# The bucket one-hots of the block building, made by GpSimd in place of VectorE

## The reference

```python
def _hypergraph_conv(x, node_idx, edge_idx, D_inv, B_inv, W, b):
    xt = x @ W
    e = B_inv[:, None] * segment_sum(xt[node_idx], edge_idx, NUM_HYPEREDGES)
    out = D_inv[:, None] * segment_sum(e[edge_idx], node_idx, NUM_NODES)
    return out + b
h = relu(_layernorm(x));  x = x + conv(relu(conv(h, W1, b1)), W2, b2)      # node_idx = src, edge_idx = dst
h = relu(_layernorm(x))
e = silu(silu(concat([h[src], h[dst], weight]) @ eW1 + eb1) @ eW2 + eb2)
x = x + silu(concat([h, segment_sum(e, src)]) @ nW1 + nb1) @ nW2 + nb2
```

## Time and profile before

| | us |
|---|---|
| median of 3 runs | 13558.7 |
| lowest and highest | 13548.79 and 13559.01 |
| the profiled execution | 13559.45 |
| its span, from first to last instruction | 13557.3 |

### The profile page before, as it was taken

How to read it: one execution, slowest core, us unless ns; L and a number is a source line. 1 busy time by engine, 2 the same in 40 slices (tenths; PEclk the granted TensorE clock), 3 DMA queues, 4 the chain that set the end, 5 groups by cost and what they waited for, 6 DMA issues and landing times. The chain is left out here.

```text
span 13557.3 us, 345638 instructions
## 1 busy us (share of the span) xinstructions
PE 12400.8 (91%) x120142; PEld 10602.5 (78%) x120730; DVE 7926.7 (58%) x35861; ACT 5611.8 (41%) x11943; POOL 3.1 (0%) x17
## 2 busy tenths in 40 slices
PE   4989898989898999999999799999999999999997
PEld 3777777777777789989999678888888888888886
DVE  8999999999999951122211444444444444444443
ACT  3878787878787840000000222222222222222222
POOL 0000000000000000000000000000000000000000
PEclk9999999999999999989999599999999999999998
DMA  2222222222222246657666322221122112221112
GB/s 62 71 69 71 70 71 70 71 69 71 69 71 69 71 141 190 179 143 192 187 192 192 103 68 66 66 66 64 65 66 66 66 64 66 66 66 66 65 65 67
DMA packets 804041, 1224.45 MB, mean 90 GB/s; under 512 B 164354, under 2 KB 545418, under 8 KB 802080
## 3 DMA queue, kind: packets, MB, share of 16 engines
q1 hardware_dynamic: 801008, 1209.28, 29.6%
q10 hardware_dynamic: 1840, 0.53, 0.0%
HBM read 850.92 MB, written 358.61 MB: 89 GB/s over the span
## 5 line engine op out<-in xcount | busy, mean ns | idle before, releaser
L708 ACT ACTIVATE RB<-PS 128x1024 fp8e4<-128x1024 f32 x2401 | 2436.8, 1020 | 738.1 <-PE PS L588 736.2
L1725 DVE TENSOR_TENSOR Zb<-p,eb2s 128x512 f32<-128x512 f32 (+1 forms) x1274 | 868.1, 681 | 2938.6 <-PE p L1642 2938.6
L1670 ACT ACTIVATE Y<-pT,eb1s 128x512 f32<-128x512 f32 (+1 forms) x1274 | 865.3, 679 | 2663.9 <-PE pT L1631 2327.6
L561 PE MATMUL S<-LH,OHf 128*102 128x256 f32 x6860 | 1624.9, 384 | 43.7 <-ACT LH L677 43.5
L1037 PE MATMUL hp<-ACC,RG 128*128 128x193 bf16 (+1 forms) x19208 | 1633.6, 246 | 6.4 <-DMA RG<-adjT 6.4
L1037 PEld LDWEIGHTS hp<-ACC,RG 128*128 128x128 fp8e4 x19208 | 1619.5, 97 | 14.1 <-issue 7.1
L1642 PE MATMUL p<-eW2s,Y 128*128 128x128 f32 x9996 | 1433.1, 287 | 0.0
L561 PEld LDWEIGHTS S<-LH,OHf 128*102 128x102 f32 x6860 | 1111.4, 170 | 354.6 <-DVE LH L794 62.7
L1654 PE MATMUL pA<-Z,Os 128*128 128x128 f32 x9996 | 1353.7, 279 | 0.2 <-ACT Z L1676 0.2
L1676 ACT ACTIVATE Z<-Zb 128x512 f32<-128x512 f32 (+1 forms) x1274 | 791.9, 622 | 1277.3 <-DVE Zb L1725 1267.2
L849 DVE TENSOR_SCALAR OU<-iot,SBk 128x256 bf16<-128x256 bf16 x4802 | 1318.5, 275 | 0.0
(11 more groups left out here) (264 smaller groups left out, 15614.4 us busy)
## 6 DMA issues: line engine op xcount, KB each, us to landing
RG<-adjT SPq DMA_DIRECT2D x1372, 224.0 KB, 3.4
adj<-RB SPq DMA_DIRECT2D x343, 448.0 KB, 2.5
adjT<-RB SPq DMA_DIRECT2D x686, 224.0 KB, 3.0
RG<-adj SPq DMA_DIRECT2D x686, 224.0 KB, 3.4
sdb<-bk SPq DMA_DIRECT2D x98, 1280.0 KB
sdb<-bk SPq DMA_DIRECT2D x98, 1024.0 KB
sdb<-bk SPq DMA_DIRECT2D x98, 832.0 KB
tab_p<-Pst SPq DMA_DIRECT2D x25, 384.0 KB, 2.7
```

What stands on the lines that cost most here:

```text
L561: ins = e.matmul(S[0:KEYS, 0:2 * P], lhsT=OHf[g % 2][:, k, :], rhs=LH[g % 2][:, k, :], start=g == 0 and k == 0, stop=g == NGR - 1 and k == ...
L708: e.activation(RB[n % NSLOT][:, :, k, :], PS[u % 2][:, :].rearrange("p (a w) -> p a w", a=2), ACT.Copy, accum_out=gs[:, u:u + 1], saturate ...
```

## The change

GpSimd's program gets a loop that makes the one-hots of all chunks, group by group, each after `v_key` (the chunk's `kd` is made) and `p_s` (the place in `OH` is free). VectorE's `onehots` is taken out at all its places. `keys(i + 1)` moves from the last group (13) to group 10 of turn i, and the VectorE wait for its result goes.

```diff
--- before.py
+++ after.py
@@ -485,6 +485,26 @@
                         e.affine_select(out=last[:, :], in_=last[:, :], compare_op=ALU.not_equal, fill=1.0, base=-(P - 1),
                                         pattern=[[0, P]], channel_multiplier=1).then_inc(c_init, 1)
 
+                        def onehots(i, g):
+
+                            if isinstance(i, int):
+                                e.wait_ge(v_key, i * 2 + 3)
+                                past(e, p_s, i * NGR + (g + 1 - NGR))
+                            else:
+                                wait_here(e, v_key, i * 2 + 3)
+                                wait_here(e, p_s, i * NGR + (g + 1 - NGR))
+                            for k in range(GT):
+                                ins = e.tensor_scalar(OH[:, g * GT + k, :], iot1[:, 0:KEYS], kd[:, g * GT + k:g * GT + k + 1], None, ALU.is_equal)
+                            ins.then_inc(v_oh, 1)
+
+                        for g in range(NGR):
+                            onehots(0, g)
+                        with e.Fori(1, NCH) as i:
+                            for g in range(NGR):
+                                onehots(i, g)
+                        onehots(NCH, 0)
+                        onehots(NCH, 1)
+
                     @block.sync
                     def _(e):
                         reg = e.alloc_register("chunk_at")
@@ -764,12 +784,6 @@
                             past(e, a_lh, i * NGR)
                             e.tensor_copy(pl[:, :, :], ld[:, 1:3, :]).then_inc(v_ld, 1)
                             e.wait_ge(v_ld, i + 1)
-
-                        def onehots(i, g):
-                            past(e, p_s, i * NGR + (g + 1 - NGR))
-                            for k in range(GT):
-                                ins = e.tensor_scalar(OH[:, g * GT + k, :], iot1[:, 0:KEYS], kd[:, g * GT + k:g * GT + k + 1], None, ALU.is_equal)
-                            ins.then_inc(v_oh, 1)
 
                         def ranks(i, g):
                             e.wait_ge(a_c, i * NGR + (g + 1))
@@ -913,12 +927,8 @@
                                 if rank:
                                     if g == 0:
                                         payload(i)
-                                    elif g + 1 < NGR:
-                                        onehots(i, g + 1)
-                                    else:
+                                    elif g == NGR - 4:
                                         keys(i + 1)
-                                        e.wait_ge(v_key, i * 2 + 6)
-                                        onehots(i + 1, 0)
                                 if unit_ and g == 0:
                                     if rank:
                                         ranks(i, g)
@@ -937,13 +947,9 @@
                                     step(i, u, before)
                             if rank:
                                 fullest(i)
-                                onehots(i + 1, 1)
                                 filled(i)
 
                         keys(0)
-                        e.wait_ge(v_key, 4)
-                        onehots(0, 0)
-                        onehots(0, 1)
                         turn(0, True, False, False)
                         turn(1, True, True, False)
                         with e.Fori(2, NCH) as i:
```

## The result

The changed kernel takes 13466.5 us (median of 4 runs, 13442.6 to 13473.5) against 13558.4: 92 us less, a ratio of 0.9931 with a 95% interval of 0.9914 to 0.9948. A later series gave 13465.6 us and 0.9924 (0.9910 to 0.9937). So the change made the kernel faster by 0.7%, where slower, 13,850 us, had been forecast as the likeliest. The range of 13,290 to 14,200 us holds the result, but only because it reached over to the other sign.

A forecast was written before the change was run, and what follows sets the result against it. VectorE was taken as the bound; 14.5 us a chunk of GpSimd's company against 8.5 won gave +6.0, x 48 = +288 us on 13559.45: 13,850 us, range 13,290 to 14,200.

The forecast's parts named there:

- The bound of before: Building stage of the unchanged kernel: VectorE, 95% busy, sets the pace at 96.4 us a chunk.
- What is removed: VectorE's one-hots: 10.9 us a chunk, 10.1 without the last call, which only lengthens the wait in `filled`.
- The company: Last four groups and chunk's end: 58 of 70 GpSimd one-hots each hold VectorE 0.25 us, 14.5 us a chunk.
- TensorE's floor: TensorE, next after VectorE, needs 88.8 us a chunk, so at most 7.6 us can be won; 4.6 taken.
- The lower end of that step: Least gain once VectorE is relieved: the 1.6 us a chunk that TensorE waits for one-hots.
- The step that was moved: `keys(i + 1)` goes three groups up; its own time doesn't change and the rest of the turn covers its waits.
- Free company: Rival, last four groups: GpSimd costs VectorE 0 to 0.15 us a one-hot; faster, 13,340 us; chance 0.34.
- GpSimd giving way: Rival: GpSimd gets in only during ranks' reads and VectorE's idle time, just keeping up; 13,410 us; chance 0.11.
- GpSimd too slow: Rival: a GpSimd one-hot takes over 1.38 us and becomes the bound; 13,970 us at 1.5 us; chance 0.05.
- The signs that I had named: Trace marks: right if VectorE stays at 95% or more, wrong if about 90% and TensorE's waits for `OU` vanish.
- The sign by durations: VectorE's lines 848 and 849 over 0.24 and 0.27 us on average, stretched only in groups 10 to 13.
- the losing forecast: Whole kernel: GpSimd holds VectorE for full instructions, net +6.0 us a chunk, slower at 13,850 us; chance 0.50.

The follow-up runs named there:

- the cut: Kernel before the change with half of TensorE's products of blocks and features left out in `sums`: 13368.3 us, ratio 0.9862.
- The company run: Kernel before the change, plus 90 unread one-hots a chunk made by GpSimd beside VectorE's untouched work: 13656.9 us, ratio 1.0069.
- late_keys: Changed kernel with `keys(i + 1)` put back from group 10 to group 13: 13466.0 us, ratio 0.9935.
- early0: Changed kernel with ScalarE scaling `LH` before taking out any of the last group's units (early = 0 for 2): 13361.9 us, ratio 0.9856.

## Why the prediction was wrong

**The bound of before** was right: VectorE, shown by the cut that leaves the chunk at 96.38 us.

**What is removed** was right: 10.9 us a chunk by the starts, 10.0 by VectorE's busy time, and of it the last call only lengthens a wait. That wait came to 6.9 us instead of 2.6, because the rest of the saving piled up there too.

**The company, 58 x 0.25 = 14.5 us a chunk, is the step that failed and turned the sign.** Two prices had no row, and I chose wrongly for both. The GpSimd instruction takes 0.54 us, not 0.25; but beside it VectorE loses 0.016 to 0.031 us, not the whole instruction. In the changed kernel even the 1.1 us a chunk that this makes are hidden in VectorE's wait. I had put the point at which the sign turns at 0.15 us, and the truth is a fifth of that or less. By the rule of the Trainium skill (SBUF — State Buffer, section "Who interferes with whom"), a VectorE `tensor_scalar` in a two-port mode and a GpSimd instruction shut each other out for the whole instruction. The company run does not agree: 90 instructions x 0.57 us stood beside VectorE in a chunk, and VectorE was late by 2.4 us. Either the rows' fast `tensor_scalar` is not of the kind that it means, or they hold the ports for a small part of their time; no run here tells which.

**TensorE's floor was mis-sized, and it set the size of the gain.** The prediction had 88.8 us a chunk, 82.2 of work and 6.6 of waits, and took 4.6 us of the 7.6 above it. The changed kernel runs at 94.5: 83.2 us of TensorE's work at full clock, 3.0 that the lower level adds to it, and 8.3 idle. So the work was short by 1.0 us. That may be what TensorE and ScalarE cost each other over `PS`; no run separates it. The other two terms, 3.0 and 1.7 us, had been left out. One is the wait for ScalarE's last `LH`, 0.9 us a chunk before and 1.7 after; the other is the time on the lower clock after the idle stretch, 2.7 us a chunk before and 3.0 after. Both could have been read from the trace of before, the one in its waits between 2000 and 3000 us, the other in the clock of 0.97 in the earlier trace rows and in the timeline, where the operation that takes 0.27 us in the earlier trace rows takes 0.42:

```profile
...
PE S L561 <- ACT LH L677: 9.0, 10, 0.9
...
```

```profile
...
2063.34 0.42 PE L586 MATMUL PS<-OU 128*128 128x256 bf16 x1
...
```

The lower end of that step, the 1.6 us that TensorE waited for one-hots, was nearly the answer (1.94), but by luck. The ten groups won 3.2 us a chunk (62.65 to 59.45 on average over the turns), and the rest of the turn lost 1.3, with the longer wait for `LH` and the clock in it.

**The step that was moved** was right at zero: late_keys.

**The rivals.** Free company was the right mechanism, at 0.34; its 13,340 us was 126 us too low, because it stood on the same floor. GpSimd giving way is out: it makes 70 one-hots in 37.5 us without a pause beside VectorE, at 0.54 us each, and in the window with the chunk's end, where VectorE waits for some 7 us, 25 take 12.88 us, 0.52 each. GpSimd too slow is out; twice the work still fits in the chunk.

**The signs that I had named** told most of it: VectorE's share down, to 87%, and TensorE's small waits gone. The sign by durations would have misled. VectorE's small `OU` is longer than before (median 256 against 243 ns between 1000 and 4000 us), as the losing forecast had it. But in the turn shown it is longer in the groups where GpSimd rests, 276 ns, than beside it, 249. The distance between starts is what told.

## What to carry to other kernels

When the busiest engine is relieved, add up the next one from instruction spacing and then add its idle ends and the time at the lower clock behind them: without these last two the floor came out 6% too low. A gap between two engines of 90% and 95% busy is worth a few us a chunk, however much is taken off the first; the larger gain here, 104 us from one line of ScalarE's order, was in the chunk's end, and two thirds of it came only after VectorE had been relieved. Where three engines are busy for 93, 97 and 100% of a stretch, to relieve one of them brings little and tells little. Where a term without any row decides the sign, its two ends are both forecasts; a small kernel that puts the disputed work beside the unchanged one prices it directly.

## What the runs showed of the hardware

- A GpSimd `tensor_scalar` of 128x102 bf16 with one number per partition takes 0.54 us, against 0.16 us from start to start on VectorE; a cast of 128x128 took 0.25.
- Beside it, VectorE lost 0.027 us per GpSimd instruction in the run where it was the bound (0.031 by its busy time) and 0.016 in the changed kernel; GpSimd itself lost 0.02 us (0.54 against 0.52).
- TensorE's clock falls to its lower level after nearly every chunk's idle end: in the changed kernel the low stretches begin 4 to 17 us after the cast at line 819, in 47 of 48 turns. With the same TensorE work, 4.0 (early0), 5.9 (changed kernel) or 8.4 us (no work for GpSimd) of a chunk's busy time fell on that level, at a price of 2.0 to 4.2 us.
- An edit in one stage took 95.5 us of idle time out of another stage's loop and 185 us of its time on the lower clock, 190 us together, since a us there costs half a us. A cut kernel's total is not a measure of its stage; its pace is.
